# Strings of steps that run on across the borders of rounds, in a two-layer attention and expert kernel on one core

## What is computed

```python
x = x + xattn0(layernorm(x), ctx)              # one wide head, softmax over 256 keys
y = layernorm(x)
o = y + attn(norm(y), heads=32, width=8) @ wo
x = x + gelu(o @ w1[e]) @ w2[e]                # expert fixed by the batch
x = x + xattn1(layernorm(x), ctx)              # softmax over the token itself and 256 keys
y = layernorm(x)
h = y + attn(norm(y), heads=16, width=16) @ wo
x = x + h + moe(norm(h))                       # 8 experts, top 2 of all 4096 tokens, relu
```

## Time and profile before

| | us |
|---|---|
| median of 3 runs | 2061.82 (2059.59 to 2388.49) |
| the profiled execution | 2058.43 |
| its span, first to last instruction | 2056.6 |
| start until the first step of round -1 | 31.5 |
| rounds -1 to 1 (three) | 31.5 to 208.2 |
| rounds 2 to 13 | 208.2 to 1307.3, 91.6 each |
| rounds 14 to 17 | 1307.3 to 1656.3 |
| the experts part | 1656.3 to 2056.6 |

### The profile page before, as it was taken

The page is one execution under the profiler, slowest core; times in us unless marked ns, Lnnn a source line. Parts: engine busy times, 40 slices in busy tenths (PEclk is TensorE's granted clock), DMA queues, the critical chain, the costliest instruction groups (busy, mean ns, idle before and its releaser), DMA issues. The chain is left out here.

```text
span 2056.6 us, 37550 instructions
## 1 busy us (share of the span) xinstructions
PE 1890.6 (92%) x13657; PEld 1445.2 (70%) x13657; DVE 1353.9 (66%) x3466; ACT 994.1 (48%) x1956; POOL 606.2 (29%) x490
## 2 busy tenths in 40 slices
PE   5699999999999999999999999999887659999998
PEld 4466767777766767677776777766666439999997
DVE  2456667676767767675766767676765457677664
ACT  1255556565556556555655656655343223333332
POOL 0102131221303121220313121230223046777674
PEclk8789999999999999999999999999989759999999
DMA  5223441515244351514344251414120254444231
GB/s 191 87 88 124 139 159 65 175 55 170 100 131 145 122 175 50 174 65 159 122 151 152 73 175 55 165 60 149 59 78 11 72 178 91 119 91 88 43 44 25
DMA packets 205704, 224.86 MB, mean 109 GB/s; under 512 B 15083, under 2 KB 195248, under 8 KB 205520
## 3 DMA queue, kind: packets, MB, share of 16 engines
q1 hardware_dynamic: 191136, 206.40, 30.3%
q0 software_dynamic: 14384, 16.06, 4.8%
HBM read 150.82 MB, written 72.52 MB: 109 GB/s over the span
## 5 line engine op out<-in xcount | busy, mean ns | idle before, releaser
L1270 DVE TENSOR_REDUCE MX<-bank 128x2 f32<-128x512 f32 x768 | 493.1, 683 | 200.4 <-PE bank L903 199.4
L1519 ACT ACTIVATE PT<-bank 128x512 f32<-128x512 f32 x768 | 417.6, 598 | 228.9 <-PE bank L940 227.6
L903 PE MATMUL bank<-KS,QS 32*128 32x256 f32 (+1 forms) x1536 | 194.6, 332 | 45.2 <-DMA QS<-q_dram 26.0
L955 PE MATMUL bank<-PT,VA 128*32 128x256 f32 x3072 | 214.1, 398 | 5.4 <-ACT PT L1519 2.3
L903 PEld LDWEIGHTS bank<-KS,QS 32*128 32x128 f32 (+1 forms) x1536 | 120.5, 193 | 124.9 <-DVE MX L1270 44.4
L940 PE MATMUL bank<-QM,KS 32*128 32x256 f32 (+1 forms) x1536 | 194.5, 332 | 9.8 <-ACT PT L1519 8.7
L1872 ACT ACTIVATE hid<-bank,b1T 128x512 f32<-128x512 f32 x128 | 87.8, 686 | 227.8 <-PE bank L1824 227.8
L748 POOL TENSOR_TENSOR rrC<-uwC,cst 128x4 f32<-128x4 f32 x16 | 16.3, 1019 | 583.1 <-DVE uwC L1239 583.1
L940 PEld LDWEIGHTS bank<-QM,KS 32*128 32x128 f32 (+1 forms) x1536 | 119.0, 190 | 95.7 <-ACT PT L1519 45.5
L1837 PE MATMUL bank<-W2h,hTh 128*128 128x256 f32 x512 | 142.7, 279 | 0.0
L1837 PE MATMUL bank<-W2l,hTh 128*128 128x256 f32 x512 | 141.4, 276 | 0.0
(11 more groups left out here) (331 smaller groups left out, 3865.4 us busy)
## 6 DMA issues: line engine op xcount, KB each, us to landing
W<-in_L_ffn_w_dram SPq DMA_DIRECT2D x48, 1024.0 KB, 7.4
KS<-k_dram SPq DMA_DIRECT2D x64, 512.0 KB, 6.9
QS<-q_dram SPq DMA_DIRECT2D x64, 512.0 KB, 8.3
k_dram<-qTQ SPq DMA_DIRECT2D x32, 256.0 KB, 2.5
q_dram<-pTQ SPq DMA_DIRECT2D x32, 256.0 KB, 2.7
k_dram<-PRP SPq DMA_DIRECT2D x32, 256.0 KB, 2.5
q_dram<-cTP SPq DMA_DIRECT2D x32, 256.0 KB, 2.8
X<-in_x_dram SPq DMA_DIRECT2D x16, 256.0 KB, 7.0
```

The lines of the kernel that those rows point to most:

```text
L903: x = mm(halves(u)[:, r, :], Q[strip, slot, r * P:(r + 1) * P], K[strip, slot, :], start=True, stop=True)
L955: x = mm(bank[4][SLOT * j:SLOT * (j + 1), 0:D], V[:, kc, n * per:n * per + SLOT], PT[:, n % 8, kc, :], start=kc == 0, stop=kc == 1, tile_p ...
L1270: v.tensor_reduce(MX[:, slot % 4, j, :], halves(u), AX, ALU.max, negate=True).then_inc(h.maxed, 1)
L1519: s_.activation(PT[:, n % 8, :, :], halves(2 + n % 2), ACT.Exp, scale=h.scale).then_inc(h.exp, 1)
```

## The change

There is no border any more. The threads of all rounds are chained, one long thread for each letter, and the texts are read one after the other; a text may use more or fewer letters of a thread than a round has. FIRST replaces the implied text of round -1 and the texts of rounds 0 and 1; FOURTH replaces those of rounds 14 to 17. ORDER is still used 12 times with the same count of each letter (24 S, 8 T, 24 E, 12 V, 28 P, 19 Q), but it starts where FIRST left the threads: S 10 steps ahead of the round, P 8, E 5, T 4, V 1, Q none. So all six letters have another order in it. `shared`, which holds what bank 4 waits for, is one dictionary for all rounds, so a step waits for the step that really stood before it.

```diff
-ORDER = "QQSPPQSPPQTSPQSPESTQPESPPESPTSPSEVSPTESVESPPTSEPQSPEVSEPQSEVPQESVEQTPQSEPSEQVPSEQVPSETPESQVEQSPEQVESPQTPPEQPEVEVEQV"
+ORDER = "PPPPQQSVESPPQSPQSPEVSEPQTPESQVESQPSEPQVPTQESPQSEPPQESVEQPVPTESQPEPSEVQSEVPETPQEQSVESQESVETSQVESTPPESQPESTPESVPSEPTS"
...
-    def round_(r, par, b=True, p=True, a=True, d=True, order=ORDER):
-        running = threads(r, par, b, p, a, d)
+    rounds = [(-1, 1, False, False, True, False), (0, 0, True, False, True, False), (1, 1, True, True, True, False)]
+    rounds += [(r, r % 2, True, True, True, True) for r in range(2, n - 1)]
+    rounds += [(n - 1, 1, True, True, False, True), (n, 0, False, True, False, True), (n + 1, 1, False, False, False, True)]
+    parts = [threads(*each) for each in rounds]
+    running = {name: chain(*(part[name] for part in parts)) for name in parts[0]}
+    for order in (FIRST, SECOND, THIRD, *[ORDER] * (n - 4), FOURTH, EARLY, LATE, LAST):
         for name in order:
             next(running[name])
...
+            shared = {}
+
             def threads(r, par, b_, p_, a_, d_):
                 hd, hb = lined_up(r, b_, d_)
-                last = hd[1] if hd else hb[1] if hb else None
-                shared = {}
-                if last:
-                    h, b = last
-                    shared = {"os": (h.os, now(t, b * h.groups + h.groups)), "shifted": (h.shifted, now(t, b * h.twos + h.twos))}
```

More of the change, by code:

```diff
@@ L121 @@
 N_R = 1 + N_ROUTE * 2
[L124 to L127, removed]
@@ L128 @@
-LATE = "RRPSPPSPSPTSEPETRRPSREPPRESRRQVPRQTSRQQPERVRRPESRPPTRPQQEVSEVSSSESRSSPQPQVSQPVQVESQPSEVPEQTPPVEQESQPQERRRQETESRQPRPRERERRRRREETQQSSEPPRVVRRRSVESPTE"
-LAST = "SSSPTQQSPPESETSQEPVSETSQQPEPVQETSEPVEQPPVEESVSVVSTQSPSQPEPQPESQEPEESVVPTPPQPEQQQSPETSEVQSEPPPQSPPEPSEQESPVEEVTPQSSP"
-def schedule(n, threads):
-    def round_(r, par, b=True, p=True, a=True, d=True, order=ORDER):
-        running = threads(r, par, b, p, a, d)
+FIRST = "STESEQSESQSPSQPTESPQQSSSPPVEEESSPQPQEPETPSSTQEPEVVVQPSSSSTPQEVSSEVPPSVQEPPPPQQPTSVQESQSSSPESEQPPPTVEPSPEETQPEQQPTQVESPSPSVEEVPPEPQPEPVEPETEQQSSPETVTPSEPSPQSSETPVSVEPQSESEVSEPTSESQPESPVESVEPSPTQESVQEPQQSEQSPSQQQQETQPSTPVSEQPEVEPQSEPPTSEPTQPVSPVPEPPESTQPSQPEVSPQEPSPSVPVSTVEPPSPEPEPQSPSPESPSQTEPPQSVPSEPTESPEVSPEQQQQSQPEQQVPEPSEPEQVQPTEQVESEPSEVSETSEVSEQVETPPESQPTESPSVPSEPTS"
@@ new lines @@
+SECOND = ""
+THIRD = ""
+FOURTH = "PPPQQPQSEVSPQTESQPPQEVSPQSPVSEQSPEQSETPSEPQVQESPQESTPQEVQPEVQVQEPSPQSEPPQSEPEQTEPVRRPREVRRQSERVSESTQSVESPPETPERRRQSPQTQESPVSERVSEPRRSPRTSPRSRPPSTPESRSEVSEQQPRTQPEVSEQPVSQPSEQPSQESPQEPSQEVSPQRRERRVRPRRRTQPEVEQRRPRRESPRVPRTPEPERERRVSERRPVRESRPVSTPPEQQSPEQRQTPESVRPSRQRREPTQQSPRRRPPESRPSPSTRPEVQRSSEPEVTSVVEEQPQQPSSQPQSQESPPQTPEQSPESSQVTESQQSEVQRERRPQERPRPRERREPRRRPRRVTSEQRERRSVVPQSPVEEESSPTPQSPESPETSPETPPVSEVPSEVPEPSPTSQSEQQTQTPVSQEEVPSEPPPVSEVSPPEEPSQQVVPVQSVSEPEQVEETPQPTSVEPEEPEEESQQQSESSPQPQQS"
@@ new lines @@
+EARLY = ""
+LATE = ""
+LAST = ""
+def schedule(n, threads):
+    rounds = [(-1, 1, False, False, True, False), (0, 0, True, False, True, False), (1, 1, True, True, True, False)]
[4 more added lines that the diff above has]
+    for order in (FIRST, SECOND, THIRD, *[ORDER] * (n - 4), FOURTH, EARLY, LATE, LAST):
@@ L142, in round_ @@
         for name in order:
             next(running[name])
[L145 to L153, removed]
 class Routes:
```

## The result

| | before | after |
|---|---|---|
| median of the runs beside each other | 2064.03 us (2059.59 to 2388.49) | 2034.97 us (2029.42 to 2042.48) |
| the profiled execution | 2058.43 | 2029.42 |
| its span | 2056.6 | 2027.6 |

The ratio is 0.987, with a 95% interval of 0.982 to 0.991: 1.3% less time, within the 2% that count here as no change. In a second set of runs the same kernel took 2029.1 us, ratio 0.984 (0.978 to 0.989). The execution of 2388.49 us was a slow one: it is in the median and the range of before, but not in the ratio.

The account below looks back on a forecast made before the run. PE in written order bounds the kernel: 87.0 us own work plus 4.6 of waits a steady round. Gains of 23 (steady), 4 (first), 5 (last) and 1 (pairs there) make 33 us: 2061.8 becomes 2029, range 2000 to 2056.

Parts of the forecast that it names:

- Steady rounds: Rounds 2 to 13: 1.9 us a round gained, from 91.6 to 89.7, or 23 us in twelve.
- Pairs: Steps S and E in steady rounds: new neighbours cut PE's own work from 17.0 to 16.3, gaining 0.7 us a round.
- The fetch of width 16: Steady rounds: QS fetch no longer behind the puts of width 8, S0 waits less, gaining 1.2 us a round.
- The norm of D1: Steady rounds: NP directly after the moments just meets the product needing it, gaining 0.5 us a round.
- New tight places and the old cluster: Steady rounds: new close spots at P25, P21 and S19 cost 0.9 us; waits of the round-end cluster save 0.4.
- The lower clock: Steady rounds: short spells at TensorE's lower clock reckoned at 0.9 us a round, no gain put on them.
- First rounds: Rounds -1 to 1: of 55 us lost, 4 taken back, 0 to 10, as later work begins early.
- Last rounds: Rounds 14 to 17: of 100 us, 5 taken back, between 15 lost and 20 gained; pairs there 1 us.
- (a): Rival, chance 0.13: the norm NP on VectorE slowed by GpSimd's own norm, 18 us of gain go: 2047 us.
- (b): Rival, chance 0.22: tight places all met, S0 waits for nothing, 3.6 us a round gained: 2004 us.
- (c): Rival, chance 0.16: VectorE's queue makes equal new waits, only pairs and ends gain, 12 us: 2050 us.
- (d): Rival, chance 0.06: fetches take today's 12.5 us from product, S0 and S8 wait more: slower, 2097 to 2105 us.

Follow-up runs that it names:

- experiment 5: Changed kernel with four pairs of a step S and a step E on different rows of the array taken apart in ORDER; 2070.39 us, ratio 1.006.
- experiment 2: Kernel before with one letter of ORDER moved: product for v of width 16 (and its fetch) ahead of product for q of width 8; 2043.15 us, 0.991.
- experiment 4: Kernel before with product for v of width 16 ahead of q of width 8, and norm of D1 one score step earlier; 2052.84 us, 0.997.
- experiment 8: Changed kernel with the old texts for rounds -1, 0 and 1, then 28 letters bridging to the new ORDER; 2030.84 us, ratio 0.986.
- Experiment 9: Changed kernel with FOURTH replaced by letters still due in its first round, then the old texts of rounds 14 to 17; 2046.06 us, ratio 0.994.
- experiment 3: Kernel before with the norm of D1 moved right behind the moments, ahead of two score steps; 2099.92 us, ratio 1.019.
- experiment 1: Changed kernel's chained threads and single bank 4 dictionary, but with the old strings end to end, keeping the old instruction order; 2061.35 us, ratio 1.001.
- experiment 6: Changed kernel with score step S0 moved ahead of the logits, nearer to the product for q of width 16; 2080.26 us, ratio 1.012.

## Why the prediction was right

The time said was 2029 us, measured 2035; for the profiled execution 2025 was said and 2029.4 came. But part of it is luck, two misses that cancel: the steady rounds gained 14 us more than I reckoned, and the head lost 12 where I had a gain of 4.

**Steady rounds: 1.9 us a round said, 3.1 measured** (36.7 us in place of 23; the other 1.8 of the 38.5 is the step that moved over the mark).

- *Pairs*: 0.7 said, 0.7 measured (the rest of 87.9 against 87.2 over the eleven whole rounds). The rest holds waits in the middle of steps too, so this is the pairs and what such waits changed. The prices of 0.43, 0.44 and 0.67 are those of the trace of before; experiment 5 puts 0.49 on a split pair.
- *The fetch of width 16*: 1.2 said, 1.27 measured as idle time (15.2 us in twelve) and 1.1 in experiment 2. The chain was right in its parts too: QS issued 5.9 us behind the product (said 5.3), landed after 4.8 (said 4.8). S0 waits 0.25 a round, 0.4 to 0.5 said.
- *The norm of D1*: 0.5 said, 0.8 measured (9.5 us to 0.2). PE doesn't wait since the tight chain of 4.4 and PE's work of 4.35 do meet, as reckoned, and a step E ahead, which itself waits 0.22, can give the rest; I haven't tested that.
- *New tight places and the old cluster*: -0.9 and +0.4 said. The four small waits that now lead come to 0.84 a round, but they aren't those I named: P25 costs PE nothing that the profile shows as idle, though its weight load does wait for the copy by ACT, as I had expected (row below), and 0.2 each fall on the transposition of the maxima (L915, once for ACT's copy OS and once for MT), a shifted score and the product at L1143. Of the old ones only PE's wait for PT can be compared, 4.1 us to 2.6, or 0.12 a round. All idle time together fell by 1.54 a round (34.5 to 16.0).

PEld's wait at the product after the norm, rounds 2 to 13:

```profile
PEld bank L849 <- ACT nTP L1499: 7.1, 12, 0.6
```

- *The lower clock*: this was the term that lacked. I saw 0.9 a round as "a short spell of the lower clock" and put no gain on it. It is 20.5 us before and 0 to 6.8 in the new order where neither pairs nor S0 were touched, a gain of 0.85 (0.6 in the second profile). With 1.54 of idle time and 0.7 of the rest that is 3.1, the measured sum. What brought this gain stays open. Only one of the four spells of before follows a long wait (2.9 us for QS). The other three begin 71 to 72 us into a round, with no wait of PE over 0.3 us in the 10 us ahead of them, behind a row of short steps (a pair of S and E, ND, V, E, the logits, S, E, NQ). All ten spells of experiments 2 and 4 begin at 69 to 72 us too. The new order has other neighbours there; no run moved them alone. Over the whole program nothing was gained: 201.3 us at the lower clock before and 195.9 after, since the head has more of it.

The window of PE's short steps in round 4 of before and the one behind it (PE's granted clock is the 1.00 and the 0.50):

```profile
449.00:461.30 12.30, 12.20 (x119) 8.78 (x122) 9.98 (x33) 7.68 (x17) 3.68 (x4) 1.00 0.08 23
461.30:468.10 6.80, 6.73 (x33) 4.76 (x26) 4.23 (x9) 3.57 (x8) 5.87 (x5) 0.50 0.21 78
```

**First rounds: +4 said, 12 lost.** The sign was wrong. I had weighed only what blending saves there; 22 us of work of later steps (24 by my reckoning for experiment 8) run in the head, where there is little to set beside them and the granted clock is 0.82 (0.85 before). In this profile the clock costs some 10 us more than before and idle time 3; the time at the lower clock differs by 20 us and more between profiles with the same FIRST. The mean start of round 2 says the same: 240.5 us in six kernels, against 207.0 in the five with the old head, 33.5 more for 22 of work. Experiment 8 shows that no text is to blame: with the old letters and a bare bridge of 28 steps round 2 begins at the same time within this scatter. So the 12 us go with running ahead, as both texts tried have it; a better bridge isn't ruled out. At 3.1 a round they are paid back in four rounds.

**Last rounds: +5 and 1 for pairs said, some 4 measured** (24.3 less, of which 20 is work done ahead). The chain from NP to S0 kept its length (18.7 and 18.8 us). The stretch from the product v of batch 15 to the experts, which I said would stay at 52.8, fell to 47.7; but 3 of these 5 us are the mark, since that product now stands nearer to S0 (4.4 us ahead of it, before 7.4). From S0 to the experts it is 43.3 us, before 45.4: 2 us. Experiment 9 says that FOURTH matters, by up to 10 us.

**The rivals.** (a) *The norm meets GpSimd* falls. NP is at 410 ns, and it is POOL that pays, as round 1 had shown: the half of its own norm beside which VectorE's runs takes 1.53 us, the other 1.2, and the mean over both rose from 1253 to 1358 ns. The slow NP of before has another cause: of its 32 records the 26 of 967 to 1478 ns ran at least in part beside POOL's sums H and RES, which read two tiles, and the other six, of 407 to 515, beside POOL's norm alone, which reads one. In the new order H and RES come 9 us later behind X. The Trainium skill, GPSIMD Engine Reference, section 1 (Specifications), names as the cause of contention what kind the VectorE instruction is; here it is one and the same VectorE instruction at 410 and at 1350 ns, and the kind of POOL's decides. I have this from reading the records of all kernels, not from a run that moved H alone. POOL in the round of the earlier trace rows, where NP runs from 738.43 to 740.68:

```profile
737.97 1.28 POOL L797 TENSOR_TENSOR H<-H,rowb 128x512 f32<-128x512 f32 x1
739.21 1.32 POOL L798 TENSOR_TENSOR RES<-X,XP 128x512 f32<-128x512 f32 x1
740.51 2.46 POOL L754 TENSOR_SCALAR X<-X,mvD,rrD 128x256 f32<-128x256 f32 x2
```

(b) *All covered* came close in the steady rounds: 1.3 us idle are left, and 88.4 (88.5 over whole rounds) was nearer to its 88 than to my 89.7. It failed at the head. (c) *The waits only move* falls for this order, and holds for the old one (experiments 3 and 4). Its remark that the chaining itself does nothing is what experiment 1 shows. (d) *The fetches are too near* didn't come, but its mechanism is real: 2 us nearer and the kernel is 1.2% slower than before (experiment 6), with a price double the wait for the clock that I hadn't in it. By its own terms (1.7 of waits, 1.4 gained elsewhere) it would decide from 3.1 us of waits, not from 3.5.

What follows for the change: threads that run over the borders aren't needed for the largest single term. One letter in the old order brings 15 us of the median, 19 of the profiled span (experiment 2), where the whole change brings 27 to 29: half to two thirds. The rest is better neighbours, the norm with scores far enough around it, and in the steady rounds less time at the lower clock. I haven't tried those in an order that keeps its borders.

## What to carry to other kernels

Where one engine walks a written order, cost an edit to it by two counts: what the engine's own steps take beside their new neighbours, and the distance in its work from each producer to its consumer against the chain between them. Moving a step earlier on a shared queue saves only if what is queued behind can bear the wait (experiments 3 and 4); take the slack from the queue, not only from the step. And count a recurring wait of 2 us on TensorE at about double, if the granted clock falls after it as it did in experiment 6; the clock also fell without any wait, so look in each kernel at what stood ahead of a spell. Running ahead costs once at the head, so it pays only over enough rounds.

## What the hardware showed

- Waits of about 2 us that come back in each round went with the lower clock, though PE was busy 96 to 97% of the time: 95.6 us in twelve rounds with two of 1.5 to 2.0 in each (experiment 3), 44.4 with one of 1.9 (experiment 6). In experiment 6 all eleven spells began 1.2 to 2.2 us behind the end of S0's wait; in experiment 3 all fifteen began during such a wait or within 1.6 us behind its end.
- A wait is not needed for it. In experiment 5 all seven spells (23.9 us) began 0.7 to 1.6 us behind a wait of only 0.46 us. In experiments 2 and 4 none of the ten spells (20.5 and 41.0 us) had a wait of PE over 0.3 us in the 10 us ahead of it, and in the kernel before (20.5) only one of four had.
- The same norm of 256 columns on VectorE took 401 to 414 ns in 30 of 32 records beside GpSimd's norm of one SBUF input (after; the other two, in the last rounds, 564 and 622), and 967 to 1478 in the 26 records that ran at least in part beside GpSimd's sums of two (before); GpSimd's norm took 1.53 us beside VectorE's, 1.2 alone.
